# Products that nobody reads, put on TensorE in the lead of attention

## What is computed

```python
x = x + minimal_gru(layernorm(x))       # W_hg, sigmoid gates, a scan over the tokens, W_out
h = layernorm(x)
x = x + ffn(h)
# ffn(h):
a = layernorm(h) * g + b
q, k, v = heads(a @ Wq), heads(a @ Wk), heads(a @ Wv)      # 16 heads of 8
attn = softmax(q @ k.T / sqrt(8))                          # 256 x 256 per sequence and head
h = h + (attn @ v) @ Wo
m = layernorm(h) * g2 + b2
w, idx = top_2(softmax(m @ Wg)); w = w / sum(w)            # 8 experts
return h + sum_k w_k * (gelu(m @ W1[idx_k] + b1) @ W2[idx_k] + b2)
```

## Time and profile before

| | us |
|---|---|
| median of 3 runs | 1054.08 |
| lowest and highest | 1046.05, 1059.02 |
| the profiled execution, timed | 1052.99 |
| its span from first to last instruction | 1051.1 |

### The profile page before, as it was taken

One profiled execution on the slowest core, in us unless ns is written; L12 is line 12 of the kernel. 1 busy time (PEld: TensorE's weight loads), 2 busy tenths in 40 slices (PEclk: granted clock), 3 DMA queues, 4 the chain that ended last, 5 costly groups with the idle time before them and its releaser, 6 DMA issues.

```text
span 1051.1 us, 25392 instructions
## 1 busy us (share of the span) xinstructions
PE 787.5 (75%) x8366; PEld 484.2 (46%) x8367; DVE 804.0 (76%) x1600; ACT 583.0 (55%) x1198; POOL 529.8 (50%) x669
## 2 busy tenths in 40 slices
PE   3777746588998989898879888834999999994000
PEld 2455534323444444343424344322888888884000
DVE  7788779686886798989887989156888888888512
ACT  6745358625765678787646778722555555552000
POOL 9600089600225372625118587843777146665775
PEclk9999889955987899999968999966999999998555
DMA  7820013411211111211011221102555445553432
GB/s 188 306 102 1 1 41 127 168 47 42 58 42 41 38 52 53 66 36 39 18 32 42 60 65 55 34 5 56 134 132 137 103 116 131 129 128 100 122 82 73
DMA packets 132071, 84.16 MB, mean 80 GB/s; under 512 B 54520, under 2 KB 117628, under 8 KB 131982
## 3 DMA queue, kind: packets, MB, share of 16 engines
q1 hardware_dynamic: 123790, 66.20, 21.8%
q0 software_dynamic: 8192, 16.79, 6.0%
HBM read 30.25 MB, written 41.94 MB: 69 GB/s over the span
## 4 chain that ended last, share of the span: by engine, by line
PE 60%; DVE 10%; POOL 9%; ACT 8%; issue 8%; DMA 1%; ACTq 0%; SPq 0%; POOLq 0%; DVEq 0%
PE bank L1337 57%; ACT arena L855 5%; POOL HT L757 3%; POOL Z L757 3%; DVE arena L1036 2%; PE bank L1341 1%; POOL rr L497 1%; PE bank L1517 1%; DVE arena L1100 1%; POOL xh L501 1%; DVE Z L1020 1%; DVE mom L955 1%; ACT arena L765 1%; DVE Z L1027 1%; ACT Z L806 0%
## 5 line engine op out<-in xcount | busy, mean ns | idle before, releaser
L1100 DVE TENSOR_REDUCE arena<-bank 128x2 f32<-128x512 f32 x512 | 329.8, 685 | 77.5 <-PE bank L1337 75.2
L855 ACT ACTIVATE arena<-bank 128x512 f32<-128x512 f32 x512 | 285.9, 594 | 136.0 <-PE bank L1337 134.8
L1337 PE MATMUL bank<-QK 31*128 31x256 f16 (+1 forms) x2048 | 183.7, 295 | 56.4 <-ACT arena L855 31.3
L1337 PE MATMUL bank<-w2p,QK 128*128 x1280 | 216.5, 246 | 1.4 <-DVE arena L1300 1.4
L928 ACT ACTIVATE arena<-bank,b1s 128x256 f32<-128x256 f32 x320 | 125.3, 475 | 102.4 <-PE bank L1337 99.9
L1337 PE MATMUL bank<-arena,w1h 128*128 128x256 f16 x640 | 166.3, 277 | 10.4 <-DMA arena<-expert_in 8.9
L689 POOL DMA_INDIRECT expert_in<-HT,idx x128 | 133.2, 1041 | 71.7 <-issue 35.9
L1337 PE MATMUL bank<-arena,VA 128*32 128x256 f32 x2048 | 151.7, 418 | 0.7 <-ACT arena L855 0.7
L1337 PEld LDWEIGHTS bank<-QK 32*128 32x128 f16 (+1 forms) x2048 | 52.0, 94 | 191.0 <-ACT arena L855 145.6
L1337 PEld LDWEIGHTS bank<-w2p,QK 128*128 128x128 f16 x1280 | 124.0, 98 | 10.7 <-issue 1.7
L1295 DVE TENSOR_TENSOR QK<-arena,QK 128x1024 f16<-128x1024 f32 x80 | 98.0, 1225 | 2.7
(11 more groups left out here) (158 smaller groups left out, 1152.5 us busy)
## 6 DMA issues: line engine op xcount, KB each, us to landing
QK<-qk_parts SPq DMA_DIRECT2D x96, 128.0 KB, 2.7
expert_in<-arena SPq DMA_DIRECT2D x40, 256.0 KB, 3.2
expert_out<-arena SPq DMA_DIRECT2D x80, 128.0 KB
qk_parts<-arena SPq DMA_DIRECT2D x16, 512.0 KB, 2.8
X<-x SPq DMA_DIRECT2D x8, 512.0 KB, 5.9
wst<-w SPq DMA_DIRECT2D x16, 256.0 KB, 2.8
out<-arena SPq DMA_DIRECT2D x16, 256.0 KB, 2.6
expert_in<-HT,idx POOLq DMA_INDIRECT x128
```

The source lines that it names most:

```text
L855: nc.scalar.activation(PT[t % 8], bank[3 + t % 2][:, :], ACT.Exp, scale=DH ** -0.5)\
L1100: V.tensor_reduce(nmax[n % 2][:, :, 4 * j + g], bank[u % 3][:, :].rearrange("p (q t) -> p q t", q=2), AX.X, ALU.max, negate=True).then_inc ...
L1337: return nc.tensor.matmul(dst, lhsT, rhs, start=start, stop=stop)
```

## The change

Ahead of the lead, PE issues 24 products of `w3h` (queries' part, 128 x 128, float16) with `htg[0]` (high halves, 128 x 512) into the whole of bank 6. In the lead it issues four more of them behind each of the steps 3, 7, 11, 15, 19 and 23. They stand behind the two waits for the evacuated group 14 and wait for nothing else. Nobody reads what they write.

```diff
             pe.wait_ge(lo_ready, NG - 1)
             pe.wait_ge(v3_ready, NG - 1)
+            def warm(n):
+                for _ in range(n):
+                    mm(bank[6][:, :], w3h[:, 0, :], htg[0][:, 0, :])
+
+            warm(24)
             for u in range(LEAD):
                 scores(0, u, False, True)
+                if u % 4 == 3:
+                    warm(4)
                 if u == 17:
                     max_t(0)
             pe.wait_ge(lo_ready, NG)
```

## The result

The changed kernel takes 1056.29 us (median of 20), the kernel before 1047.76 (20, among them the three shown above). The ratio is 1.0084, 95% interval 1.0057 to 1.011: slower by 8.8 us, 6.0 to 11.5, which is under 2% but clear of the noise. The forecast was 1058, against a profiled execution of 1052.99, so a loss of 5.4.

A forecast was written before the change was run, and what follows sets the result against it. No engine bounds the kernel everywhere; DVE's maxima pace the lead, a DMA wait precedes it. Span 1051.1 + 0 for the 24 + 5.4 for the fours + 1.9 gave 1058.4, said as 1058 us, range 1053 to 1064.

The forecast's parts named there:

- Down through the lead: Main forecast: clock falls in or soon after the wait's remaining gap and stays down through the lead; chance 0.57.
- the full-clock sum: Lead, fours at full clock: 1.6 us from a bank coming free against DVE's 1.81 in hand, so no stall.
- The 24 cost nothing: Wait for QK rows: 24 products take 5.8 us, covered by the DMA wait, leaving 1.6 to 2.1 us idle.
- The term of the four at half clock: Lead: each four takes 2.7 us against DVE's 1.81, so DVE stands 0.9 us, six times, 5.4 us.
- The sum: Whole program: 1051.1 + 0 + 5.4 + 1.9 = 1058.4, said as 1058 us, with early attention as before.
- The size of full clock: Early attention: 28 steps take 21.1 us at full clock in place of 30.85; about 10 us at most in the stage.
- rival 2: Lead and early attention: the clock holds through both, time 1043 us; chance 0.20.
- the gap: Wait for rows: 1.6 to 2.1 us idle left before thin score pairs; clock falls in or soon after it.
- the row that I took for the price of a gap: At 326.7 us PE waits 2.58 us for POOL's xh; clock 1.00 up to 331, then 0.50 for several stretches.

The follow-up runs named there:

- the holds: Kernel before plus 34 products in the wait and filling in the lead, most also in the first six attention steps; ratios 1.0015, 0.9956, 0.9983, with b1_shift filling 0.9932.
- the first lighter hold: Kernel before plus 34 products in the wait, filling behind every second lead step and the first six attention steps; first measurement, ratio 0.9956.
- the repeat: The first lighter hold's kernel measured again on the third chip against the kernel before; ratio 0.9983 (0.9946 to 1.002).
- 34 alone: Kernel before plus 34 products of 128 rows filling the wait for rows, nothing in the lead; ratio 0.9990 (0.9942 to 1.0038).
- 24 with a dense lead: The first lighter hold's kernel with 24 products in the wait instead of 34; one execution of 1071.74 us, kernel before 1042.75 to 1060.13.
- the 31 rows: Kernel before plus 34 products of 512 columns using 31 array rows in the wait, nothing in the lead; ran once, no time given.
- the first hold: Kernel before plus 34 products in the wait, one and a half behind every lead step, one behind each of the first six attention steps; ratio 1.0015.

## Why the prediction was right

**Down through the lead** (chance 0.57): right. The fall came 3.2 us after the rows and not in the gap, so the first group of four ran at full clock, and there DVE had no break, as the full-clock sum said. Had it come at the rows, as in another run, all six groups would have run at half clock.

**The 24 cost nothing:** right, by the trace (block and 2.14 us left, I had 1.6 to 2.1) and by the run with them alone.

**The term of the four at half clock** was too small: 0.9 us each forecast, 1.26 measured. Its parts in the row from 220.35 are 0.54 to the first product (I had 0.42), 1.82 for the four (1.68) and 0.64 from the next score to its maximum (0.61), 3.00 against 2.7; the rest is 0.06 us from the end of the maximum that frees the bank (220.29) to the score. What DVE had in hand, 1.80 us, was as forecast (1.81). The 0.12 and the 0.14 are for the most part the changes from 31-row to 128-row products and back, which the sum left out. Against that, five groups and not six made DVE stand, since the first ran at full clock. The two errors met by luck: 5.4 forecast, 5.85 in the breaks and 5.7 in the lead measured.

**The sum:** 1058 forecast from an execution of 1052.99, a loss of 5.4; measured 8.8, interval 6.0 to 11.5. Lead and early part together lost 6.1 in the profiled executions, at the interval's lower end. The remaining 2.7 us were not placed; a loss of about 6 is still within what was measured. That the median, 1056.29, lies so near the forecast of 1058 is luck in part: the base was 1054 of three runs and is 1047.8 of twenty, and the forecast loss on that base would give 1053.2. A base too high and a loss too small made up for each other.

**The size of full clock:** 21.1 us for the early part, measured 20.99 in four runs and 20.75 in the one without filling there. That it would reach the end of the program, 1043 in rival 2, is what the holds do not bear out.

**What is given back later.** The results name the mean granted clock of each run, and 2 x (1 - clock) x span is the time at half clock: in the median 261 us before and 217 for the first lighter hold, 44 less, though the stretch at half clock from 208 to 259 us, 51 us long, is gone from its trace. On the chip of the repeat it is 314 against 291, 23 less. So more time at half clock arose elsewhere, 7 and 28 us. In the 17 runs of before on the first lighter hold's chip a least-squares line gives 0.35 us of span for each us at half clock (correlation 0.94). By that, as an estimate, 7 us cost 2.5 and leave 7.5 of the 10; the medians show 3.6, the interval 1 to 8. And 28 us cost 10 and leave nothing; measured are 2 us, the interval from 6 faster to 2 slower. Both lie within wide intervals, which is all that can be said for the account. The first lighter hold's own trace, of the fastest of its runs, does not show it: behind 262 us it has 185 us at half clock, where the trace of before has 191. That part of the gain is given back in later dips is therefore argued and not shown, and whether an attention that starts at full clock falls more often for a reason was not settled.

**The reason in the text that was weakest** was the gap. I took it and the thin score products together. The runs separate them, one trace each: either is enough (34 alone falls without a gap; 24 with a dense lead falls with 2.23 us of gap). Which of the two lost the clock in the changed kernel, where it outlived the gap by 3.2 us, is open. And the row that I took for the price of a gap, the 2.58 us at 326.7, is weaker than I read it: in the traces of 34 alone, of the 31 rows and of the first lighter hold PE has no such wait before these transposes, and the clock falls behind them all the same, at 329.5, 336.2 and 321.9 us, 6.6 to 6.8 us after they start where it was 1.7 before, and for 6.8 to 6.9 us where it was 13.6. By the advice of the Trainium skill ("TensorE: Matmul & The Clock Gate", section "Why this matters for your kernels"), which is to leave no long idle gap between bursts, the changed kernel would have kept its clock. The traces disagree: it was lost with gaps of 2.14, 2.21 and 2.23 us, and with none in the 34 alone.

## What to carry to other kernels

Filling for the clock must be judged by two things apart: where the clock is worth something, and what the filling delays. Here it sat in a stage that another engine paced, and at half clock four products in a row outlasted the three banks that hid PE from that engine; spread behind every second step, with less in each place, the same idea cost nothing while the clock held (a lead of 15.59 us) and 7.6 us more than before where it did not (23.32). A partial filling is not a partial gain: with a gap of 2 us left the clock was lost, and the filling behind it ran at half clock and only cost. And what a stage gains, 10 us here, has to be looked for again at the end of the program, where 1 to 6 us are what both measurements allow.

## What the runs showed of the hardware

- Products with 31 of 128 rows did not hold the clock: 34 of 512 columns back to back, PE shown busy throughout, lost it in the wait at 206.5 us (one execution), where the same with 128 rows held it in six traces. The busy share of the profile does not tell them apart.
- Going from 31-row score products to 128-row products and back costs PE about 0.1 us each way at full clock: a step of the first hold takes 0.75 us where the columns make 0.53.
- Score products of 31 rows that are ready together run side by side: in the changed kernel six products of 256 columns take 0.62 us from 222.71, as long as two take from 220.35 (0.60), both at half clock.
- A filling that held 1.00 through the lead stayed at 0.50 in the run that entered the lead with a gap, from 213.1 us until after the early part.
- The chips differ by up to 6% for the kernel before. In the six traces from the two slower ones three of the rounds of 16 steps late in attention take 18 to 23 us, which take 13.0 to 14.5 in the other six traces, and from attention's last output product to the end pass 388 to 392 us in place of 364 to 366. The cause is open.
